# Two of twelve places of value products in an attention step are given up, and their products stand behind those of another place

## The reference, cut to what matters

```
q, k = apply_rope(q), apply_rope(k)
attn = einsum('bqhd,bkhd->bhqk', q, k) * scale
attn = where(causal mask, -1e9, attn)
attn = softmax(attn, axis=-1)
out  = einsum('bhqk,bkhd->bqhd', attn, v)
```

## Time and profile before

| | |
|---|---|
| median of 3 runs | 915.86 us (915.84 to 917.67) |
| the profiled execution, its own time | 918.87 us |
| its span, first to last instruction | 917.1 us |
| TensorE busy | 877.4 us (96%) |
| VectorE busy | 611.0 us (67%) |
| ScalarE busy | 530.8 us (58%) |
| GpSimd busy | 316.1 us (34%) |

### The profile page before, as it was taken

The page is one execution under the profiler, slowest core; times in us unless marked ns, Lnnn a source line. Parts: engine busy times, 40 slices in busy tenths (PEclk is TensorE's granted clock), DMA queues, the critical chain, the costliest instruction groups (busy, mean ns, idle before and its releaser), DMA issues. The chain is left out here.

```text
span 917.1 us, 20463 instructions
## 1 busy us (share of the span) xinstructions
PE 877.4 (96%) x6655; PEld 516.3 (56%) x6656; DVE 611.0 (67%) x1147; ACT 530.8 (58%) x1328; POOL 316.1 (34%) x465
## 2 busy tenths in 40 slices
PE   6999969999999999999999988999999999999995
PEld 4555423333333333333333323668999999999994
DVE  5878999888888888888888801777533343333342
ACT  4667337777888877787887786325333333333330
POOL 9999643333232233322223331335211111111111
PEclk9999969999999999999999999999999999999998
DMA  7578533422311222211124020746655555555550
GB/s 271 171 225 262 176 110 128 162 71 71 95 51 52 71 70 70 69 40 49 59 71 162 9 87 8 266 134 209 217 198 172 178 177 180 190 191 172 178 172 1
DMA packets 54115, 120.31 MB, mean 131 GB/s; under 512 B 9753, under 2 KB 37018, under 8 KB 47770
## 3 DMA queue, kind: packets, MB, share of 16 engines
q1 hardware_dynamic: 49482, 101.97, 35.8%
q0 software_dynamic: 4560, 17.39, 5.2%
HBM read 96.16 MB, written 23.17 MB: 130 GB/s over the span
## 5 line engine op out<-in xcount | busy, mean ns | idle before, releaser
L804 ACT ACTIVATE arena<-ps_pair 128x512 f32<-128x512 f32 (+3 forms) x768 | 329.0, 493 | 102.2 <-PE ps_pair L1136 97.4
L893 DVE TENSOR_REDUCE B_block_max<-ps_item 128x8 f32<-128x1024 f32 x288 | 340.6, 1220 | 40.8 <-PE ps_item L1043 37.5
L1136 PE MATMUL ps_pair<-q_stack,k_stack 99*128 99x512 bf16 (+7 forms) x768 | 191.3, 334 | 5.0 <-ACT arena L804 2.9
L719 POOL TENSOR_SCALAR_AFFINE_SELECT arena<-arena 128x256 f32<-128x256 f32 x256 | 104.4, 408 | 202.1 <-ACT arena L804 199.9
L1152 PE MATMUL ps_pair<-arena,B_v_quad 128*32 128x512 f32 (+3 forms) x1536 | 163.6, 498 | 1.0 <-ACT B_oacc L818 0.7
L1136 PEld LDWEIGHTS ps_pair<-q_stack,k_stack 99*128 99x128 bf16 (+1 forms) x768 | 54.0, 97 | 187.7 <-ACT arena L804 172.2
L1744 PEld LDWEIGHTS C_bank<-arena 128*128 128x128 f32 x1248 | 145.3, 192 | 3.4 <-ACT arena L1414 1.3
L1744 PE MATMUL C_bank<-arena 128*128 128x128 f32 x1248 | 145.8, 275 | 1.0 <-ACT arena L1414 1.0
L1763 PE MATMUL C_ps_p<-arena 128*128 x624 | 141.0, 379 | 0.0
L1400 ACT ACTIVATE arena<-C_bank,ffn_columns 128x128 f32<-128x128 f32 x156 | 44.7, 368 | 142.7 <-PE C_bank L1744 142.7
L1763 PEld LDWEIGHTS C_ps_p<-arena 128*128 128x128 f32 x624 | 115.6, 190 | 14.2
(11 more groups left out here) (171 smaller groups left out, 739.8 us busy)
## 6 DMA issues: line engine op xcount, KB each, us to landing
arena<-in_w_exp SPq DMA_DIRECT2D x39, 1024.0 KB, 5.1
qk_parts<-arena SPq DMA_DIRECT2D x32, 384.0 KB, 3.5
q_stack<-qk_parts SPq DMA_DIRECT2D x96, 128.0 KB, 2.9
k_stack<-qk_parts SPq DMA_DIRECT2D x64, 128.0 KB, 2.9
arena<-in_w_exp POOLq DMA_DIRECT2D x8, 1024.0 KB, 6.6
rows<-payload SPq DMA_DIRECT2D x39, 130.5 KB, 2.1
arena<-in_x SPq DMA_DIRECT2D x8, 512.0 KB, 5.2
arena<-in_x_feat SPq DMA_DIRECT2D x8, 512.0 KB, 6.0
```

Of the source, the lines that this page charges most:

```text
L719: pool.affine_select(out=block_p, in_=block_p, compare_op=ALU.is_ge, fill=0.0, base=0, pattern=[[0, 2], [1, P]], channel_multiplier=-1).th ...
L804: act.activation(pr[s % PR][:, h, 0:QW - off], ps_s[(QH * s + j) % R][:, 0:QW - off], ACT.Exp, scale=scale).then_inc(s_e, 1)
L893: dve.tensor_reduce(bmx[:, g:QH:GH, first:first + 3 * gap + 1:gap], src[:, :, :].rearrange("p c (b n) -> p c b n", n=P), AX.X, ALU.max).th ...
L1136: pe.matmul(ps_s[(QH * s + j) % R][:, 0:QW - off], ks[rows, r, half, bass.ds(g * SEQ + kb * P, P)], qs[rows, r, half, bass.ds(g * SEQ + c ...
```

## The change

Two entries of `PV_AT` move. The value products of s = 10 (of the quad before) stood at gap 27 and now stand at gap 31, directly in front of those of s = 11. The value products of s = 2 stood at gap 43 and now stand at gap 47, directly in front of those of s = 3. Nothing is added or removed; the waits in front of each `pv` are the same.

```
-        PV_AT = ((3, 2), (6, 2), (11, 2), (15, 2), (18, 2), (23, 2), (27, 2), (31, 2), (35, 2), (39, 2), (43, 2), (47, 2))
+        PV_AT = ((3, 2), (6, 2), (11, 2), (15, 2), (18, 2), (23, 2), (31, 3), (31, 2), (35, 2), (39, 2), (47, 3), (47, 2))
```

## The result

The changed kernel takes 923.19 us in the median of 6 runs (920.92 to 926.34), the kernel before, on the same chips, 916.38 us (914.98 to 918.13, 6 runs). The ratio is 1.0076, with a 95% interval from 1.0059 to 1.0093: slower by 5.4 to 8.5 us, 7.0 by the ratio. I had forecast 8.0 more.

What follows compares the result with a forecast made beforehand. TensorE was taken to set the pace, with VectorE and ScalarE close behind. 14 x (0.15 + 0.39) = 7.56, plus 0.96 for step 15, less 0.54 for the load, made 8.0 us: 915.86 to 923.9 us, range 920.3 to 927.0.

Steps and rivals of the forecast that it cites:

- TensorE sets the pace, the helpers stand close behind: Attention, 200 to 500 us: TensorE busy 299.56 of 300 us, VectorE at 88%, ScalarE at 80%, so neither has much room.
- First stretch: item12 waits for item10's reduction: Gaps 27 to 31: only 0.32 of the removed 0.57 us can be used; the stretch gets 0.15 us longer per step.
- Second stretch: score products 5,0 and 5,1 wait for exponentials 4,1 and 4,2: Gaps 43 to 47: only 0.09 of the removed 0.57 us can be used; the stretch gets 0.39 us longer per step.
- The border between two sets: Where a moved set meets its like, one change of kind goes: 0.09 us saved, bounds 0 to 0.15; set takes 0.48.
- Nothing is given back later in the step: After gaps 31 and 47 all three engines move on by the same delay; a step goes from 26.87 to 27.41 us.
- The odd steps: Step 0 has only the second stretch, taken as nothing; step 15 has no items and pays 2 x 0.48, 0.96 us.
- The wait for quad 15's stack: Item0 of step 14: loads land when they did, TensorE comes 0.54 us later, so the wait shrinks: -0.54 us once.
- the saved changes of kind alone: Rival: helpers have room, so the 30 moved sets give 30 x 0.09 = 2.7 us, time 913.2 us; chance 0.07.
- only ScalarE's place costs: Rival: the first stretch has room and gives 0.09 us a step; 4.9 us slower in all, 920.7 us; chance 0.09.
- only VectorE's costs: Rival: score 5,1 is free, so only the first stretch costs; 1.3 us slower, 917.1 us; chance 0.05.
- the border costs more: Rival: waits between paired sets, or ScalarE left dry; nothing saved at borders, 2.7 us more, 926.6 us; chance 0.08.

Runs made afterwards that it cites:

- light kernels: Orders of before and after, with reductions reading 64 of each 128 keys and exponentials writing at most 256 columns from quad 1; steps 26.703 and 26.433 us.
- light_after: The changed kernel with reductions reading 64 of each 128 keys and exponentials at most 256 columns from quad 1; step 26.433 us, against 26.703 in the before order.
- first_only: Against the kernel before, only the set of s = 10 moved, gap 27 to gap 31; step 26.974 us against 26.867, time ratio 1.0012.
- red_after: The changed kernel with only the reductions lighter, reading 64 of each 128 keys; step 27.076 us, against 26.757 in the before order with the same reductions.
- second_only: Against the kernel before, only the set of s = 2 moved, gap 43 to gap 47; step 27.220 us against 26.867, time ratio 1.0051.
- first_early: Against the kernel before, only the set of s = 11 moved up to gap 27, behind s = 10; step 26.781 us against 26.867.
- first_early_timed: The kernel of first_early again, on another chip and timed against the kernel before; step 26.780 us, time ratio 0.9994.
- exp_before: The kernel before with only the exponentials lighter, at most 256 columns written from quad 1 on; step 26.815 us against 26.867.

## Why the prediction held, step by step

- **TensorE sets the pace, the helpers stand close behind.** Held. In both light kernels TensorE has the same work, and the step falls by only 0.16 us in the order of before, but by 0.89 in the order of after. Waits and savings are right as sums too: the waits come to 0.54 + 2 x 0.09 = 0.72 us a step by the forecast, and to 0.453 + 0.27 = 0.72 by light_after.
- **First stretch: item12 waits for item10's reduction.** Held: 0.24 us of wait, and item12 starts 0.05 us behind the reduction. The stretch got 0.107 us longer (first_only); 0.15 was forecast. One thing was overlooked: I called the buffers in this stretch free except item10's, but score 1,1 waits 0.04 us for exponential 0,2. VectorE's longer wait hides it here, and red_after shows it (0.11).
- **Second stretch: score products 5,0 and 5,1 wait for exponentials 4,1 and 4,2.** Held: both start 0.06 us behind them. It got 0.353 longer (second_only); 0.39 was forecast. OUTT stands 337.73 - 315.65 = 22.08 us behind its MAXT in second_only, 0.08 less than before; 0.09 was forecast.
- **The border between two sets.** This term was mis-sized. I put 0.09 us saved, with bounds of 0 and 0.15. A pair takes 0.79 us in the traces, and the two sets apart took 0.57 + 0.36 = 0.93, so 0.14 is saved; light_after gives 0.135. That is almost all of the fixed part of a set, not the change of kind alone. Two borders at 0.05 more make the 0.09 us by which the step is shorter than forecast.
- **Nothing is given back later in the step.** Held: score 5,3 is 0.45 us later in its step than before, the next MAXT 0.453, and the halves add up.
- **The odd steps.** For step 15 I had added 0.96 us. From the start of the last MAXT to that of the last output transpose the traces have 37.752 before and 38.620 after, 0.87, which is two sets at 0.43 (0.79 - 0.36), and each half alone has half of it (38.190 and 38.191). From the second MAXT to the third lie 27.215 us before and 27.520 after: 0.31 more, where I had 0.54, so there a part was hidden that I had not seen. From the first to the second lie 25.705 before and 25.543 after, where I had no difference. That says nothing of the change: in the 14 us behind the first MAXT TensorE's granted clock was 0.56 in the mean before and 0.61 after (it rises from 0.50 to 1.00 on the way, 12.4 and 11.1 us behind that MAXT).
- **The wait for quad 15's stack.** This term failed. I had the wait 0.54 us shorter. In the profiled execution of after it is not there at all: step 13 to 14 takes 27.316 us, where before it took 29.207. But this says little of the change. first_early and first_early_timed are the same kernel, and one trace has a step of 30.434 us there, the other 26.780. So the wait comes and goes between executions, the step is longer by 0 to 3.9 us (exp_before has 30.752 - 26.815), and this should have been a spread around the forecast and no term of it. Without it the sum would have been 8.5: that it brought the sum nearer to the measured time was luck.

The sum with the measured terms, 13 x 0.453 + 0.31 + 0.87 = 7.1 us (step 0 left out), agrees with the 7.0 us of the timed runs. The profiled executions differ by less, 921.5 - 917.1 = 4.4 us in span: the one of before held 2.3 us of the stack wait, and the one of after none.

Of the rivals, the saved changes of kind alone fell with the rows of item12 and score 5,0, and it is what happens once the helpers are light. That only ScalarE's place costs falls with first_only (0.107 us more a step), that only VectorE's costs with second_only (0.353 more), and that the border costs more with light_after, where it saves 0.135. The saving of the borders is outweighed in each step, where waits of 0.72 us stand against the 0.27 us of light_after. The Trainium skill (TensorEngine Tiling (Array Packing), Key Properties) has TensorE drain at a change of tiling mode; that fewer such changes save time agrees with the 0.135 us, but whether a drain is all of it no run shows.

## What to carry to other kernels

An engine that is busy for 99.9% in the average can still owe that to the order of its work. Before a block is moved away from a place, look at when the buffers of the instructions behind it come free: if the block covered a helper's time, its removal saves little there (0.33 and 0.08 of 0.57 us here), and the block is paid at the new place, less what its border saves (0.43 us here). A pair of like blocks did save its border in these kernels (0.14 us), so form it at the place that needs the cover, and check where the next wait then stands.

## What had not been expected of the hardware

- Two sets of value products back to back cost 0.14 us less than the two apart, where a score product pays only 0.09 for being followed by another kind (0.31 against 0.22 us).
- The time at which 14 DMA loads of a stack have landed differs between executions of one kernel. First_early has 30.434 us from the MAXT of step 13 to that of step 14 in one trace and 26.780 in the other, while the steps from 2 to 13 take 26.78 in both. Timeline of TensorE in the first, then the busy time by stretch (columns as above):

```profile
497.20 0.39 PE L1136 MATMUL ps_pair<-q_stack,k_stack 128*128 128x512 bf16 x1
499.72 0.61 PE L1043 MATMUL ps_item<-k_stack,q_stack 64*128 64x512 bf16 x2 [2.13 <-DMA k_stack<-qk_parts]
...
499.72:503.00 3.28, 3.28 (x11) 0.69 (x15) 1.92 (x2) 1.58 (x3) 0.00 (x0) 0.50 0.64 265
```

- Of these 3.65 us more only 2.20 are the wait (499.72 - 497.20, less the 0.32 from score 5,3 to item0 in the other trace). The rest is a lower clock behind it: from 499.72 to 503.00 the granted clock is 0.50, the level of 1.2 GHz, after TensorE had stood idle for 2.13 us, and from item0 to MAXT it needs 4.30 us, where the other trace, at 1.00, has 2.84. In the trace of before an idle time of 2.27 us was followed by no fall of the clock: there the same way takes 504.68 - 501.83 = 2.85.
